# A fused cross-attention block on one core: GpSimd adds the half sums of the softmax once more, VectorE sums 256 columns instead of 512, and the order inside the step changes

## Chip, cores and metric

The kernel runs on one core of a Trainium2 chip. The metric is the device time of one execution in microseconds (us). Shown are the median of three runs, and one profiled execution with its own time.

## What is computed

For each of 16 batches, 1024 query rows of 512 numbers attend to 64 context rows, with 16 heads of 32:

```python
xq  = ada_ln(x_q,  t_vec, Wss_q,  bss_q)
xkv = ada_ln(x_kv, t_vec, Wss_kv, bss_kv)
q      = (xq @ Wq + bq).reshape(B, Lq, nh, dh)
k, v   = split((xkv @ Wkv + bkv).reshape(B, Lkv, 2, nh, dh))
attn   = softmax(einsum('bqhd,bkhd->bhqk', q, k) / sqrt(dh), axis=-1)
out    = einsum('bhqk,bkhd->bqhd', attn, v).reshape(B, Lq, H)
return x_q + (out @ Wp + bp)
```

The change touches the sum inside the softmax: for each row and head, 64 exponentials are added up.

## The kernel before

The query rows are cut into 128 units of 128 rows, 8 units to a batch. Products are made in float16 with each operand split into a high and a low half, so three products stand for one.

After a start of some 125 us (modulation, keys and values of all batches, the first units) the kernel is a software pipeline. One step `step(b, i)` handles the unit `i` of batch `b` and, at the same time, later and earlier units. Each engine has its own list of parts for a step, written by hand, and works it off in that order. An engine that waits in one part holds up everything behind it on its list. The engines meet only by semaphores. In step i:

- TensorE (PE): scores of unit i (`score`, L1465), weights times values of unit i-3 (`weigh`, L1487), query projection (`project`, L1442), transposition of the normalised rows of unit i+8 (`turn_x`, L1425), output projection of unit i-3 (`project_out`, L1503). `weigh` waits for both halves of the transposed weights (`pT_landed`) and for the low halves of the rows turned in the step before (`xT_done`). The change leaves PE's list as it is.
- VectorE (DVE): maximum of the scores (`score_max`, L1091), low half of the weights of unit i-2 (`split_p`, L1107), `turned_o` (L1058), scores minus maximum (`softmax_shift`, L1099), sum of unit i-1 (`weight_sums`, L1066), `turned_x` (L1051), reciprocal (`denominators`, L1073), low half of the queries (`query`, L1116), division by the sum (`normalise_p`, L1083).
- ScalarE (ACT): high half of the weights (`split_p`, L691), `turned_o` (L651), output copy (`output`, L667), row sums and squares (L710, L717), `query` (L702), `turned_x` (L643), exponentials (L726), and in steps 2 to 5 the high half of the next batch's weights (`scaled_wq_hi`).
- GpSimd (POOL): bias onto the residual row (`residual`, L503), `half_sums` of unit i-1 (L534), which adds the two halves of the 64 exponentials of each head (512 sums from 1024), the row statistics (`moments`: L479, L482), in steps 3 to 6 `scaled_wq_lo` (L541) and in steps 2 to 5 `scaled_wq` (L517) for the next batch, `add_rows` (output plus residual, L527), `normalise` (rows of unit i+9, L494).
- SyncE (SP) issues all transfers of a step from one queue: the two transposing transfers of the weights of unit i-2 (`turn_p`, L358), the residual row (`load_xr`, L342), the store of unit i-4 (L348), the rows of unit i+12 (`load_x`, L327). Step 7 begins with four copies of the next batch's keys (`copy_keys`, L369), step 2 with two of the values (`copy_values`, L380).

`load_xr(i-1)` waits until the store of unit i-5, which used the same buffer, has landed. `load_x(i+12)` waits for POOL's `normalise` of unit i+8. `copy_keys` waits for the scores of step 7. The steps of batches 1 to 13 run in a loop on the compute engines; the others are written out.

Of the kernel before, what the change touches and what calls it, by code (L numbers as in the profile page):

```python
# [5 lines left out]
ALU = mybir.AluOpType  # L6
# [8 lines left out]
P = 128  # L15
# [6 lines left out]
def adaln_cross_attention(nc, x, ctx_in, cond, Wq, bq, Wkv, bkv, Wp, bp, Wss_q, bss_q, Wss_kv, bss_kv, out):  # L22
# [19 lines left out]
    with ExitStack() as ctx:  # L42
        def sb(name, shape, dt, stack=ctx):
            return stack.enter_context(nc.sbuf_tensor(name, shape, dt))
# [4 lines left out]
        def sem(name):  # L49
            return ctx.enter_context(nc.semaphore(name))  # L50
# [105 lines left out]
        with ExitStack() as scratch:  # L156
# [3 lines left out]
        ctx_kept = sb("ctx_kept", [P, 2 * H], F32)  # L160
# [62 lines left out]
        half_done, den_done, rden_done, norm_done, pv_mm, oT_hi_done, oT_done = (  # L223
            sem(n) for n in ("half_done", "den_done", "rden_done", "norm_done", "pv_mm", "oT_hi_done", "oT_done"))
# [72 lines left out]
        def _(sp):  # L297
# [84 lines left out]
            def step(b, i):  # L382
                if i == 7:
                    copy_keys(b + 1)
                if i == 2 and b > 0:
                    copy_values(b)
                turn_p(b, i - 2, 0)
                turn_p(b, i - 2, 1)
                load_xr(b, i - 1)
                store(b, i - 4)  # L390
                load_x(b, i + 12)
# [41 lines left out]
        def _(pool):  # L433
# [95 lines left out]
            def half_sums(b, off):  # L529

                if exists(b, off):
                    wait(pool, exp_done, upto(b, off))
                    wait(pool, den_done, unit(b, off))
                    pool.tensor_tensor(half_den[:, :, :], pr[:, off % 2, :, 0:LKV // 2], pr[:, off % 2, :, LKV // 2:LKV],  # L534
                                       ALU.add).then_inc(half_done, 1)

# [20 lines left out]
            def step(b, i):  # L557
                residual(b, i - 4)
                await_rows(b, i + 9)
                half_sums(b, i - 1)  # L560
                moments(b, i + 9)
                await_moments(b, i + 9)
                if 3 <= i <= 6:
                    scaled_wq_lo(b + 1, i - 3)
                if 2 <= i <= 5:
                    scaled_wq(b + 1, i - 2)
                add_rows(b, i - 4)
                normalise(b, i + 9)

            def prime():  # L570
# [36 lines left out]
                half_sums(0, 0)  # L607
                half_sums(0, 1)
                key_lo(6)
# [8 lines left out]
        def _(act):  # L618
# [117 lines left out]
            def step(b, i):  # L736
                split_p(b, i - 2)
                turned_o(b, i - 3)
                output(b, i - 4)
                if i == 4:  # L740
                    query_bias(b + 1)
                sum_rows(b, i + 10)
                query(b, i + 4)
                turned_x(b, i + 8)
                sum_squares(b, i + 10)
                exponential(b, i)
                if 2 <= i <= 5:
                    scaled_wq_hi(b + 1, i - 2)
# [138 lines left out]
        def _(dve):  # L887
# [173 lines left out]
            def weight_sums(b, off):  # L1061

                if exists(b, off):
                    wait(dve, half_done, upto(b, off))
                    wait(dve, rden_done, unit(b, off))
                    dve.tensor_reduce(den[:, :], half_den[:, :, :], AX_X, ALU.add).then_inc(den_done, 1)  # L1066
# [52 lines left out]
            def step(b, i):  # L1119
                score_max(b, i)  # L1120
                split_p(b, i - 2)
                turned_o(b, i - 3)
                softmax_shift(b, i)
                weight_sums(b, i - 1)
                turned_x(b, i + 8)
                denominators(b, i - 1)
                query(b, i + 4)
                normalise_p(b, i - 1)

# [477 lines left out]
```

## Time and profile before

| | |
|---|---|
| median of 3 runs | 1062.99 us (1062.55 to 1064.18) |
| profiled execution: its time | 1062.06 us |
| profiled execution: its span | 1060.2 us |
| busy in the span: PE, DVE, POOL, ACT | 1019.4, 989.8, 832.3, 787.5 us |
| mean granted clock of TensorE | 0.994 of full speed |

The span runs from the first to the last instruction of the profiled execution; its time is 1.9 us longer, and the median 0.9 us above that. Busy time is a union of intervals on one engine; matmuls overlap, and their ends are modelled, so a PE that is always busy is not by that alone at its peak. The chain that ended last goes through PE for 75% of the span, through transfers for 7% and through SP's queue for 7%.

### The profile page before, as it was taken

The numbers are of one execution on the slowest core, as the hardware profiler recorded it, in microseconds if no ns is written. First come the engines' busy times: TensorE is split into PE (matmuls) and PEld (weight loads), VectorE is DVE, ScalarE is ACT, GpSimd is POOL, SyncE is SP. The second block draws the span as 40 slices with busy tenths as digits, with TensorE's granted clock in tenths as the row PEclk, the third lists the DMA queues.
The fourth block names the chain that finished last, engine by engine and source line by source line (L and its number), as shares of the span: only waits on it lengthen the run. The fifth ranks groups of instructions, "written<-read, shape, count | busy, mean of one in ns | idle before, by whom it ended". The sixth has DMA issues, their size and how long they took to land.

```text
span 1060.2 us, 29080 instructions
## 1 busy us (share of the span) xinstructions
PE 1019.4 (96%) x10051; PEld 576.6 (54%) x10051; DVE 989.8 (93%) x1288; ACT 787.5 (74%) x1400; POOL 832.3 (79%) x933
## 2 busy tenths in 40 slices
PE   6999899999999999999999999999999999999965
PEld 2666555555555555555555555555555555555532
DVE  5775899999999999999999999999999999999994
ACT  2564677878787887878787878878787878877552
POOL 2372587979888897979898888979797988889454
PEclk8999999999999999999999999999999999999999
DMA  9231478877777778777777777777777777776775
GB/s 346 102 100 51 99 175 190 178 191 183 182 193 175 184 172 197 184 176 188 194 174 183 189 182 189 169 194 183 177 188 185 183 191 177 184 191 142 160 159 129
DMA packets 382386, 185.19 MB, mean 175 GB/s; under 512 B 324828, under 2 KB 328952, under 8 KB 382344
## 3 DMA queue, kind: packets, MB, share of 16 engines
q1 hardware_dynamic: 382320, 184.66, 71.4%
q8 instruction: 22, 0.36, 0.1%
q14 instruction: 20, 0.16, 0.1%
q10 hardware_dynamic: 24, 0.01, 0.0%
HBM read 77.90 MB, written 33.55 MB: 105 GB/s over the span
## 4 chain that ended last, share of the span: by engine, by line
PE 75%; DMA 7%; SPq 7%; DVE 4%; issue 4%; POOL 2%; ACT 0%; POOLq 0%; DVEq 0%; ACTq 0%
PE ps_q L1442 26%; PE ps_o L1503 26%; PE ps_s L1465 8%; PE ps_v L1487 8%; DMA pt<-p 6%; PE ps_v L1425 4%; SPq L369 3%; SPq L358 2%; DMA cx<-in_ctx_dram 1%; PE ps_v L1296 1%; SPq L334 1%; DVE v L1023 1%; DVE p L1107 0%; DVE cx L932 0%; PE ps_s L1367 0%
## 5 line engine op out<-in xcount | busy, mean ns | idle before, releaser
L527 POOL TENSOR_TENSOR xr<-y,xr 128x512 f32<-128x512 f32 x128 | 163.0, 1273 | 57.5 <-ACT y L667 55.7
L691 ACT CAST p<-ps_t 128x1024 f16<-128x1024 f32 x128 | 129.5, 1012 | 100.0 <-DVE ps_t L1083 98.3
L534 POOL TENSOR_TENSOR half_den<-pr 128x512 f32<-128x512 f32 x128 | 163.4, 1277 | 51.1 <-ACT pr L726 49.0
L503 POOL TENSOR_TENSOR xr<-xr,bp_row 128x512 f32<-128x512 f32 x128 | 163.0, 1273 | 0.8 <-DMA xr<-in_x_dram 0.8
L1091 DVE TENSOR_REDUCE mx<-ps_s 128x16 f32<-128x1024 f32 x128 | 156.8, 1225 | 7.1 <-PE ps_s L1465 2.8
L1107 DVE TENSOR_TENSOR p<-ps_t,p 128x1024 f16<-128x1024 f32 x128 | 156.6, 1223 | 4.0 <-ACT p L691 2.7
L1083 DVE SCALAR_TENSOR_TENSOR ps_t<-pr,ps_v 128x1024 f32<-128x1024 f32 x128 | 155.8, 1217 | 0.3
L1099 DVE TENSOR_TENSOR pr<-ps_s,mx 128x1024 f32<-128x1024 f32 x128 | 155.6, 1215 | 0.1
L726 ACT ACTIVATE pr<-pr,exp_scale 128x1024 f32<-128x1024 f32 x128 | 146.3, 1143 | 10.6 <-DVE pr L1099 10.6
L702 ACT ACTIVATE q_hi<-ps_q,cur_bq 128x512 f16<-128x512 f32 x126 | 86.6, 687 | 89.1 <-PE ps_q L1442 89.1
L1503 PE MATMUL ps_o<-wp_hi,oT_hi 128*128 128x512 f16 x512 | 132.3, 381 | 13.5 <-DVE oT_lo L1058 13.5
L1503 PE MATMUL ps_o<-wp_lo,oT_hi 128*128 128x512 f16 x512 | 132.0, 380 | 0.0
L1503 PE MATMUL ps_o<-wp_hi,oT_lo 128*128 128x512 f16 x512 | 131.4, 379 | 0.0
L1442 PE MATMUL ps_q<-xT_hi,w_hi 128*128 128x512 f16 x504 | 130.7, 382 | 0.0
L1442 PE MATMUL ps_q<-xT_hi,w_lo 128*128 128x512 f16 x504 | 129.3, 379 | 0.0
L1442 PE MATMUL ps_q<-xT_lo,w_hi 128*128 128x512 f16 x504 | 129.3, 379 | 0.0
L1487 PE MATMUL ps_v<-pt,vb 128*64 128x128 f16 x3072 | 110.2, 221 | 9.5 <-DMA pt<-p 8.6
L1465 PEld LDWEIGHTS ps_s<-kb,q_hi 64*128 64x128 f16 x2048 | 80.5, 94 | 54.3 <-issue 46.6
L1465 PE MATMUL ps_s<-kb,q_hi 64*128 64x128 f16 x2048 | 108.0, 217 | 0.0
L1487 PEld LDWEIGHTS ps_v<-pt,vb 128*64 128x64 f16 x3072 | 90.2, 110 | 24.8 <-issue 14.0
L494 POOL TENSOR_SCALAR xh<-x_in,neg_mean,rstd 128x512 f32<-128x512 f32 x124 | 96.1, 775 | 1.5 <-POOL rstd L482 1.5
L1058 DVE TENSOR_TENSOR oT_lo<-ps_v,oT_hi 128x512 f16<-128x512 f32 x128 | 87.2, 681 | 6.5 <-ACT oT_hi L651 6.5
(211 smaller groups left out, 1878.4 us busy)
## 6 DMA issues: line engine op xcount, KB each, us to landing
x_in<-in_x_dram SPq DMA_DIRECT2D x128, 256.0 KB, 3.2
xr<-in_x_dram SPq DMA_DIRECT2D x128, 256.0 KB, 3.1
out_dram<-xr SPq DMA_DIRECT2D x128, 256.0 KB, 3.1
pt<-p SPq DMA_TRANSPOSE x256, 3.2
raw<-in_L_xcond_Wss_kv_dram SPq DMA_DIRECT2D x4, 512.0 KB, 5.9
cx<-in_ctx_dram SPq DMA_DIRECT2D x4, 512.0 KB, 10.9
wss_q_raw<-in_L_xcond_Wss_q_dram SPq DMA_DIRECT2D x4, 512.0 KB, 10.9
raw<-in_L_xcond_Wkv_dram SPq DMA_DIRECT2D x2, 1024.0 KB, 13.8
```

What stands on the lines that cost most here:

```text
L503: pool.tensor_tensor(xr[:, s, :], xr[:, s, :], bp_row[:, :], ALU.add).then_inc(xr_ready, 1)
L527: pool.tensor_tensor(xr[:, s, :], y[:, off % 2, :], xr[:, s, :], ALU.add).then_inc(y_ready, 1)
L534: pool.tensor_tensor(half_den[:, :, :], pr[:, off % 2, :, 0:LKV // 2], pr[:, off % 2, :, LKV // 2:LKV], ALU.add).then_inc(half_done, 1)
L726: act.activation(pr[:, off % 2], pr[:, off % 2], ACT.Exp, scale=exp_scale[:, 0:1])\
L1083: dve.scalar_tensor_tensor(out=weights, in0=pr[:, off % 2, :, :], scalar=P_UNIT, in1=rden[:, :].unsqueeze(2).to_broadcast([P, NH, LKV]), o ...
L1091: dve.tensor_reduce(mx[:, :], scores, AX_X, ALU.max).then_inc(mx_done, 1)
L1099: dve.tensor_tensor(pr[:, off % 2, :, :], scores, mx[:, :].unsqueeze(2).to_broadcast([P, NH, LKV]), ALU.subtract).then_inc(sub_done, 1)
L1107: dve.tensor_tensor(p16[:, 1, :, :], weights, p16[:, 0, :, :], ALU.subtract).then_inc(p_split, 1)
L1442: last = pe.matmul(bank[:, :], w[:, k, cols], xt[:, s, k, :], start=(n == 0), stop=(n == 3 * KC - 1))
L1465: last = pe.matmul(ps_s[:, e, P * m:P * (m + 1)], q[rows, s, m, cols], kb[rows, part, m, :, :].rearrange("p h l -> p (h l)"), start=(n == ...
L1487: last = pe.matmul(ps_v[64 * e:64 * (e + 1), 0, P * m:P * (m + 1)], vb[:, part, 2 * m + e, :, :].rearrange("p h c -> p (h c)"), pt[:, p_pa ...
L1503: last = pe.matmul(ps_o[:, :], ot[:, k, :], w[:, k, :], start=(n == 0), stop=(n == 3 * KC - 1))
```

## The change

`half_sums` stays, and a second addition on POOL follows it, `quarter_sums`: it adds the halves of the half sums (256 sums from 512) into a new buffer. VectorE's `weight_sums` then sums 256 columns. POOL's `half_sums` of a unit waits for the quarter sums of the unit before, no longer for VectorE's sum. Beside that the lists of SP, POOL, ACT and DVE get another order. PE's list stays.

```diff
+        quarter_den = sb("quarter_den", [P, NH, LKV // 4], F32)
...
             def step(b, i):
+                load_x(b, i + 12)
                 if i == 7:
                     copy_keys(b + 1)
+                load_xr(b, i - 1)
+                turn_p(b, i - 2, 0)
+                turn_p(b, i - 2, 1)
                 if i == 2 and b > 0:
                     copy_values(b)
-                turn_p(b, i - 2, 0)
-                turn_p(b, i - 2, 1)
-                load_xr(b, i - 1)
                 store(b, i - 4)
-                load_x(b, i + 12)
...
                 if exists(b, off):
                     wait(pool, exp_done, upto(b, off))
-                    wait(pool, den_done, unit(b, off))
+                    wait(pool, quarter_done, unit(b, off))
                     pool.tensor_tensor(half_den[:, :, :], pr[:, off % 2, :, 0:LKV // 2], pr[:, off % 2, :, LKV // 2:LKV],
                                        ALU.add).then_inc(half_done, 1)
+            def quarter_sums(b, off):
+                if exists(b, off):
+                    if isinstance(b, int) and unit(b, off) == 0:
+                        pool.wait_ge(v_mm, KC)
+                        pool.wait_ge(k_mm, KC)
+                    wait(pool, half_done, upto(b, off))
+                    wait(pool, den_done, unit(b, off))
+                    pool.tensor_tensor(quarter_den[:, :, :], half_den[:, :, 0:LKV // 4], half_den[:, :, LKV // 4:LKV // 2],
+                                       ALU.add).then_inc(quarter_done, 1)
...
             def step(b, i):
+                await_rows(b, i + 9)
                 residual(b, i - 4)
-                await_rows(b, i + 9)
+                moments(b, i + 9)
                 half_sums(b, i - 1)
-                moments(b, i + 9)
                 await_moments(b, i + 9)
+                quarter_sums(b, i - 1)
+                add_rows(b, i - 4)
                 if 3 <= i <= 6:
                     scaled_wq_lo(b + 1, i - 3)
+                normalise(b, i + 9)
                 if 2 <= i <= 5:
                     scaled_wq(b + 1, i - 2)
-                add_rows(b, i - 4)
-                normalise(b, i + 9)
...
             def step(b, i):
+                if i == 4:
+                    query_bias(b + 1)
+                output(b, i - 4)
                 split_p(b, i - 2)
                 turned_o(b, i - 3)
-                output(b, i - 4)
-                if i == 4:
-                    query_bias(b + 1)
                 sum_rows(b, i + 10)
+                sum_squares(b, i + 10)
                 query(b, i + 4)
+                exponential(b, i)
                 turned_x(b, i + 8)
-                sum_squares(b, i + 10)
-                exponential(b, i)
...
-                    wait(dve, half_done, upto(b, off))
+                    wait(dve, quarter_done, upto(b, off))
                     wait(dve, rden_done, unit(b, off))
-                    dve.tensor_reduce(den[:, :], half_den[:, :, :], AX_X, ALU.add).then_inc(den_done, 1)
+                    dve.tensor_reduce(den[:, :], quarter_den[:, :, :], AX_X, ALU.add).then_inc(den_done, 1)
...
                 weight_sums(b, i - 1)
-                turned_x(b, i + 8)
                 denominators(b, i - 1)
                 query(b, i + 4)
                 normalise_p(b, i - 1)
+                turned_x(b, i + 8)
```

SP's queue in step 7 of a batch, before and then with the change (kb: the next batch's keys; pt: the transposed weights; xr: the residual row; x_in: rows to come):

```order
L369 DMA kb<-k 32x8x64 [waits k_ready,s_mm]
L369 DMA kb<-k 32x8x64 x3
L358 DMA_TRANSPOSE pt<-p 128x8x128 [waits p_hi_done,pv_mm]
L358 DMA_TRANSPOSE pt<-p 128x8x128 [waits p_split]
L342 DMA xr<-in_x_dram 128x512 [waits stored2]
L348 DMA out_dram<-xr 128x512 [waits y_ready]
L327 DMA x_in<-in_x_dram 128x512 [waits xh_ready]
```

```order
L328 DMA x_in<-in_x_dram 128x512 [waits xh_ready]
L370 DMA kb<-k 32x8x64 [waits k_ready,s_mm]
L370 DMA kb<-k 32x8x64 x3
L343 DMA xr<-in_x_dram 128x512 [waits stored2]
L359 DMA_TRANSPOSE pt<-p 128x8x128 [waits p_hi_done,pv_mm]
L359 DMA_TRANSPOSE pt<-p 128x8x128 [waits p_split]
L349 DMA out_dram<-xr 128x512 [waits y_ready]
```

The loads of x_in and xr moved from behind the two transposing transfers to ahead of them; that of xr stands between the key copies and the transposing transfers.

POOL's list in a step with work for the next batch's weights (steps 3 to 5), before and then with the change:

```order
L503 TENSOR_TENSOR xr<-xr,bp_row 128x512 [waits xr_loaded1,bias_ready]
L534 TENSOR_TENSOR half_den<-pr 128x512 [waits den_done,exp_done,row_stats]
L479 TENSOR_SCALAR veps<-row_sq 128x1
L482 TENSOR_TENSOR rstd<-veps,half_neg 128x1 [waits ln_step]
L541 TENSOR_TENSOR w_lo<-w_tmp,w_hi 128x4x128 [waits w_hi_done]
L517 TENSOR_TENSOR w_tmp<-wq,cur_sc 128x512 [waits w_done]
L527 TENSOR_TENSOR xr<-y,xr 128x512 [waits xr_ready,y_copied]
L494 TENSOR_SCALAR xh<-x_in,neg_mean,rstd 128x512
```

```order
L504 TENSOR_TENSOR xr<-xr,bp_row 128x512 [waits xr_loaded1,bias_ready,row_stats]
L480 TENSOR_SCALAR veps<-row_sq 128x1
L483 TENSOR_TENSOR rstd<-veps,half_neg 128x1 [waits ln_step]
L535 TENSOR_TENSOR half_den<-pr 128x512 [waits quarter_done,exp_done]
L546 TENSOR_TENSOR quarter_den<-half_den 128x256 [waits half_done,den_done,ln_step,xT_turned]
L528 TENSOR_TENSOR xr<-y,xr 128x512 [waits xr_ready,y_copied]
L553 TENSOR_TENSOR w_lo<-w_tmp,w_hi 128x4x128 [waits w_hi_done]
L495 TENSOR_SCALAR xh<-x_in,neg_mean,rstd 128x512
L518 TENSOR_TENSOR w_tmp<-wq,cur_sc 128x512 [waits w_done]
```

One addition of 256 columns is new, directly behind the half sums and waiting for them; the row statistics moved ahead of the half sums, and the work for the weights behind `add_rows`.

DVE's list from the sum on, before and then with the change:

```order
L1066 TENSOR_REDUCE den<-half_den 128x16 [waits rden_done,half_done]
L1051 TENSOR_TENSOR xT_lo<-ps_v,xT_hi 128x4x128 [waits xT_hi_done]
L1073 RECIPROCAL ps_v<-den 128x16 [waits norm_done,den_done]
L1116 SCALAR_TENSOR_TENSOR q_lo<-ps_q,cur_bq,q_hi 128x512 [waits q_hi_done]
L1083 SCALAR_TENSOR_TENSOR ps_t<-pr,ps_v 128x1024 [waits p_split,rden_done]
```

```order
L1081 TENSOR_REDUCE den<-quarter_den 128x16 [waits rden_done,quarter_done]
L1088 RECIPROCAL ps_v<-den 128x16 [waits norm_done,den_done]
L1131 SCALAR_TENSOR_TENSOR q_lo<-ps_q,cur_bq,q_hi 128x512 [waits q_hi_done]
L1098 SCALAR_TENSOR_TENSOR ps_t<-pr,ps_v 128x1024 [waits p_split,rden_done]
L1066 TENSOR_TENSOR xT_lo<-ps_v,xT_hi 128x4x128 [waits xT_hi_done]
```

The low half of the turned rows went from between the sum and its reciprocal to the end of the step.

## Rows read from the trace of the kernel before

**Rows 1.** Busy time by stretch: us, PE, PEld, DVE, ACT, POOL (count), clock, DMA share, GB/s.
```profile
500.00:600.00 100.00, 99.69 (x1037) 56.18 (x1034) 99.20 (x123) 79.72 (x144) 85.70 (x97) 1.00 0.77 185
```

**Rows 2.** Timeline of one step, PE and DVE: start us, us, engine, line, operation.
```profile
500.01 0.86 PE L1487 MATMUL ps_v<-pt,vb 128*64 128x128 f16 x24
500.12 1.23 DVE L1091 TENSOR_REDUCE mx<-ps_s 128x16 f32<-128x1024 f32 x1
...
504.20 0.68 DVE L1066 TENSOR_REDUCE den<-half_den 128x16 f32<-128x512 f32 x1
...
505.41 0.25 DVE L1073 RECIPROCAL ps_v<-den 128x16 f32<-128x16 f32 x1
...
506.16 1.22 DVE L1083 SCALAR_TENSOR_TENSOR ps_t<-pr,ps_v 128x1024 f32<-128x1024 f32 x1
...
507.30 0.86 PE L1487 MATMUL ps_v<-pt,vb 128*64 128x128 f16 x24
```

**Rows 3.** Waits of PE between 200 and 900 us: total, times, longest.
```profile
PE ps_v L1487 <- DMA pt<-p: 1.7, 9, 0.3
```

**Rows 4.** Chain that ended last, around step 7 of two batches: start us, us, what.
```profile
506.59 0.80 PE ps_s L1465 x24
...
511.47 3.22 DMA pt<-p
514.69 0.14 issue
...
565.15 0.80 PE ps_s L1465 x24
```

**Rows 5.** SP's queue in the same step 7, with the store before it.
```profile
505.87 0.34 SPq L348 DMA_DIRECT2D out_dram<-xr  x1
...
507.40 2.65 SPq L369 DMA_DIRECT2D kb<-k  x4
510.15 2.66 SPq L358 DMA_TRANSPOSE pt<-p  x2
512.85 0.58 SPq L342 DMA_DIRECT2D xr<-in_x_dram  x1
...
513.95 0.43 SPq L327 DMA_DIRECT2D x_in<-in_x_dram  x1
```

**Rows 6.** Waits of POOL between 200 and 900 us.
```profile
POOL half_den L534 <- ACT pr L726: 35.7, 48, 1.1
POOL xr L527 <- ACT y L667: 20.7, 24, 0.9
POOL w_lo L541 <- POOL rstd L482: 10.5, 48, 0.2
```

**Rows 7.** Timeline of POOL in one step.
```profile
507.79 1.28 POOL L534 TENSOR_TENSOR half_den<-pr 128x512 f32<-128x512 f32 x1
509.15 0.19 POOL L479 TENSOR_SCALAR veps<-row_sq 128x1 f32<-128x1 f32 x1
509.43 0.55 POOL L482 TENSOR_TENSOR rstd<-veps,half_neg 128x1 f32<-128x1 f32 x1
```

**Rows 8.** Issue to landing of L358 between 127 and 131 us.
```profile
DMA to landing us min/median/max: 3.6/3.7/3.7
```

**Rows 9.** Issue to landing of L348 (stores) in the whole span.
```profile
DMA to landing us min/median/max: 2.0/3.1/4.6
```

**Rows 10.** Timeline of PE at the first steps of the pipeline.
```profile
133.65 0.86 PE L1487 MATMUL ps_v<-pt,vb 128*64 128x128 f16 x24 [2.61 <-DMA pt<-p]
```

**Rows 11.** Timeline of the last units: ACT, PE, SP.
```profile
1043.00 1.01 ACT L691 CAST p<-ps_t 128x1024 f16<-128x1024 f32 x1 [2.61 <-DVE ps_t L1083]
...
1044.07 1.03 PE L1503 MATMUL ps_o<-wp_hi,oT_lo 128*128 128x512 f16 x4
...
1045.92 2.61 SPq L358 DMA_TRANSPOSE pt<-p  x2
```

More of the change, by code:

```diff
@@ L159, in adaln_cross_attention @@
         p16 = sb("p16", [P, 2, NH, LKV], F16)
-        ctx_kept = sb("ctx_kept", [P, 2 * H], F32)
+        quarter_den = sb("quarter_den", [P, NH, LKV // 4], F32)
+        ctx_kept = sb("ctx_kept", [P, 2 * H - NH * LKV // 4], F32)
         ctx_kept1 = sb("ctx_kept1", [P, KC, 512], F32)
@@ L222, in adaln_cross_attention @@
             sem(n) for n in ("s_mm", "mx_done", "sub_done", "exp_done", "p_hi_done", "p_split"))
-        half_done, den_done, rden_done, norm_done, pv_mm, oT_hi_done, oT_done = (
-            sem(n) for n in ("half_done", "den_done", "rden_done", "norm_done", "pv_mm", "oT_hi_done", "oT_done"))
+        half_done, quarter_done, den_done, rden_done, norm_done, pv_mm, oT_hi_done, oT_done = (
+            sem(n) for n in ("half_done", "quarter_done", "den_done", "rden_done", "norm_done", "pv_mm", "oT_hi_done", "oT_done"))
         out_mm, xr_ready, y_copied, y_ready = sem("out_mm"), sem("xr_ready"), sem("y_copied"), sem("y_ready")
@@ L607, in prime @@
                 half_sums(0, 0)
+                quarter_sums(0, 0)
                 half_sums(0, 1)
+                quarter_sums(0, 1)
                 key_lo(6)
```

## The prediction

> **What bounds the kernel now.** I read the busy time by stretch first. In the middle of the run PE is busy 99.69 of 100 us, DVE 99.20, POOL 85.70 and ACT 79.72 [rows 1]: two engines look full, so busy shares do not tell which one paces. The timeline of one step does. From one `weigh` to the next PE takes 507.30 - 500.01 = 7.29 us [rows 2], and the waits of PE over 700 us come to 1.7 us, in nine places, all for the transposed weights [rows 3]. DVE has work for nearly the same 7.29 us, but no wait of PE is for DVE. So PE's own work of 7.29 us a step, 58.32 us for the 8 steps of a batch, is a floor that the change, which leaves PE's list alone, cannot lower.
>
> The chain shows what is above the floor. From the scores of step 7 of one batch to those of the next are 565.15 - 506.59 = 58.56 us [rows 4], 0.24 us over the floor. They are lost behind step 7: SP issues four key copies (507.40, 2.65 us), only then the two transposing transfers (510.15) [rows 5]; the second is issued at 511.47, lands 3.22 us later, and 0.14 us after that `weigh` starts [rows 4]. **So VectorE's saving has 0.24 us a batch to win, 3.6 us over the 15 changes from one batch to the next.** The question is what the rest of the change costs.
>
> **The change part by part.** *VectorE.* A sum over 1024 columns takes 1.23 us, one over 512 takes 0.68 [rows 2]; the line through both gives 0.40 for 256, a gain of 0.28 a step (none at all is the one bound, half of 0.68 the other). PE does not wait for it, so by itself I count it zero: PE's 7.29 us cover it. But `turned_x` goes to the end of the step, and its result lets PE's `weigh` of the next step begin. The sum starts 4.08 us after the step's first DVE row; then 0.40, some 0.03 until the dependent reciprocal, 0.75 from there to `normalise_p` as now, 1.22 for that and about 0.6 for the low half: 7.08 us. With 0.14 from signal to `weigh`, as after a landing [rows 4], that is 7.22, where `weigh` wants to start 507.30 - 500.12 = 7.18 us after the same row [rows 2]. Just in time; I take zero and keep the other end (no saving in the sum, 0.3 us late) for a rival.
>
> *GpSimd.* Its 256 column addition is not in the trace. Half of the 512 column one is 0.64 us; the line through that row (1.28) and the one column row (0.19) gives 0.19 + 256 x 1.09/511 = 0.74 us [rows 7]. I take 0.73, since a GpSimd instruction visibly has a fixed part. It waits for the half sums of the same engine: `veps` ends at 509.34 and `rstd`, which needs it, starts at 509.43 [rows 7], so 0.09 (0.22 at worst, the wait of `w_lo` for `rstd`: 10.5 us in 48 waits [rows 6]). That is 0.82 us a step, 6.6 a batch. Has POOL this room? Over 12 batches it waited 35.7 us for exponentials and 20.7 for outputs [rows 6], 4.7 us a batch; so 58.56 - 4.70 = 53.86 us are taken, fixed gaps included. The 10.5 us of `w_lo` waiting for `rstd` (0.88 a batch) go away, because the half sums now stand between. New demand: 53.86 + 6.56 - 0.88 = **59.5 us a batch, more than PE's 58.32**. Bounds: 58.1 (0.64 and no wait) to 61.5 (0.74 and 0.22 each time, nothing hidden). The waits can be used up nearly in full, since ACT's output copy now comes first in its step, and the exponential is moved ahead of `turned_x`. POOL becomes the pacing engine, at +0.98 us a batch over 58.56; in steps 3 to 5, which carry the weights' work, its sums fall behind and VectorE's sum waits for them.
>
> Here a rule bears on the result. By busy time POOL takes 85.70% of 58.56 us [rows 1], 50.2, and with eight times 0.74 it is 56.1: POOL would fit, and nothing of the 14.7 us below would come from it. By the spacing of starts it does not. The Trainium skill (Perfetto Trace Analysis, GPSIMD Engine Instruction) says that the reported spans of this engine are unreliable and that the distance from start to start is to be used; the trace shows why: half sums last 1.28 us and the next start comes after 1.36 [rows 7]. I go by spacing, and keep the other as a rival.
>
> *SyncE.* In step 7 the load of the residual row now stands between the key copies and the transposing transfers: 0.58 us and 0.04 of issue gap, 0.62 later [rows 5]. The key copies cannot start earlier, as they wait for step 7's scores; `load_x` ahead of them is 0.43 us, and POOL's late `normalise` can hold it. The landing gets longer too: with two such loads just ahead it took 3.6 to 3.7 us [rows 8] instead of 3.22 [rows 4]. Half of the difference, 0.22, is my value. So PE loses 0.84 a batch here (0.62 to 1.07). In the other steps the same loads are ahead, and the residual's load waits for the store of the step before to land: issued at 505.87 [rows 5], landing 3.1 later [rows 9], load 0.62, first transfer 1.3: the second is issued at about 510.95. At 511.47 it was 0.24 too late, so 511.23 is the last moment: 0.28 us of room, zero taken. The value copies of step 2, moved behind the transfers, have a step's rest; zero as well.
>
> *Adding up.* POOL's 0.98 and SP's 0.84 a batch are delays of two loops beside each other, PE's being late gives POOL time; I take the larger one: 15 x 0.98 = 14.7. At the first step of the pipeline, where PE already waits 2.61 us for the transposed weights [rows 10], SP now issues both loads ahead of them: 0.43 + 0.58 + 0.08 = 1.1. At the end ACT's copy of an output comes ahead of the last unit's weights: PE ends that output at 1045.10, the copy is some 0.7, the weights' high half starts at 1045.8 instead of 1043.00, ends a microsecond later, and SP's transfers, at 1045.92 before, start at about 1046.8 [rows 11]: 0.85 (between 0 and 2.8). Sum: 14.7 + 1.1 + 0.85 = 16.6 us on the profiled execution's 1062.06, **1079 us**; against the median of 1062.99 it is 16 us.
>
> **Rivals.** *SP's delay alone.* POOL's addition fits. Then 15 x 0.84 + 1.9 = 14.5 gives 1076.6, with 0.62 it is 1073.3. For it speaks POOL's busy share; against it that its gaps fill every step with `scaled_wq`.
>
> *Transfers late in every step.* The Trainium skill (DMA: Bandwidth & Descriptors, Queues, rings and completion order) says that each transfer engine takes its descriptors in ring order; loads issued ahead are then served ahead. The trace agrees in part: 3.7 instead of 3.2 us behind two loads. With the whole 0.45 in every step the room of 0.28 is gone and seven steps lose 0.17 each, step 7 loses 1.07: 2.26 a batch, 1062.06 + 33.9 + 1.9 = 1098. If VectorE's sum does not get shorter at all, so that the change does not do what it says, `turned_x` ends 0.3 us late; a late `weigh` delays the next step too, so half of it counts, 0.16 a step, 1.3 a batch beside SP's 0.84: 1096. Both decide by rows that are off by a few tenths; the half landing penalty alone keeps 0.06 us of room.
>
> *Faster.* PE's only wait goes: the second transposing transfer of step 7 would have to be issued by 511.23 instead of about 512.1, or land in 2.4 us instead of 3.22. Then 3.6 us are won, 1058.5. Nothing in the rows is that short; only that PE is full now bounds it from the other side.
>
> *No change.* POOL fits, and SP's issue of the residual load is hidden by a wait that I read wrongly (0.24 a batch stays): 1061 to 1065.
>
> **Numbers.** Forecast 0.50; SP alone 0.22; late in every step 0.13; no change 0.07; faster 0.08. The range 1061 to 1094 leaves out the faster case and the upper half of the late one. About 0.2% (2 us) is what a measurement of this kernel can tell from no change. Slower 0.85, same 0.07, faster 0.08.
>
> **What would show it.** Right: POOL's waits for exponentials and outputs shrink from 4.7 us a batch to nearly nothing; the step 7 to step 7 distance grows to about 59.5; VectorE waits for the quarter sums in steps 5 to 7; PE waits for the transposed weights after step 7 by 0.8 us or more; the sum takes 0.40 us. Wrong: PE's step stays at 7.29 with waits of POOL left, or PE waits in every step for the transposed weights or for VectorE's low half.

## The result and the profile after

The changed kernel takes 1094.27 us (median of 4 runs, 1091.85 to 1096.03) beside 1062.77 us of the kernel before (4 runs, 1061.79 to 1064.18): 1.0292 times as long, 95% interval 1.0276 to 1.0308. It is slower, as forecast, but by 31.5 us where the forecast was 16. The profiled execution, the fastest of the four, took 1091.85 us; its span is 1090.0 us (1060.2 before), the mean granted clock 0.992 (0.994 before).

Busy time in the middle of the run, to set beside [rows 1]; the columns are the same:

```profile
500.00:600.00 100.00, 98.02 (x1002) 54.68 (x1001) 93.58 (x120) 80.31 (x143) 94.21 (x109) 1.00 0.74 177
```

TensorE went from 99.69 to 98.02, VectorE from 99.20 to 93.58, and GpSimd from 85.70 to 94.21. Nothing reads 100 any more. Next, TensorE's `weigh` rows (L1502 is L1487 of before) over one batch of the changed kernel, from the timeline:

```profile
529.05 0.86 PE L1502 MATMUL ps_v<-pt,vb 128*64 128x128 f16 x24 [0.54 <-DMA pt<-p]
...
536.34 0.86 PE L1502 MATMUL ps_v<-pt,vb 128*64 128x128 f16 x24
...
543.73 0.86 PE L1502 MATMUL ps_v<-pt,vb 128*64 128x128 f16 x24
...
551.19 0.86 PE L1502 MATMUL ps_v<-pt,vb 128*64 128x128 f16 x24
...
558.48 0.86 PE L1502 MATMUL ps_v<-pt,vb 128*64 128x128 f16 x24
...
565.88 0.86 PE L1502 MATMUL ps_v<-pt,vb 128*64 128x128 f16 x24
...
573.17 0.86 PE L1502 MATMUL ps_v<-pt,vb 128*64 128x128 f16 x24
...
581.05 0.86 PE L1502 MATMUL ps_v<-pt,vb 128*64 128x128 f16 x24 [0.17 <-issue]
...
588.98 0.86 PE L1502 MATMUL ps_v<-pt,vb 128*64 128x128 f16 x24 [0.57 <-DMA pt<-p]
```

From one row to the next should be the 7.29 us of [rows 2]. Six of the eight distances are within 0.17 of it, and two are long: 7.88 and 7.93, from the seventh `weigh` to the eighth and from the eighth to the first of the next batch. The batch is 588.98 - 529.05 = 59.93 us. The second long one ends a wait for the transposed weights; what lies behind the first the chain of waits shows, in the same stretch:

```profile
571.61 1.05 POOL w_tmp L518
...
573.21 0.68 ACT y L682
573.90 0.91 ACT p L706
...
574.92 0.43 DVE p L1122
...
576.07 0.69 DVE oT_lo L1073
...
576.89 0.63 PE ps_v L1440 x4
577.52 2.59 PE ps_o L1518 x12
580.11 0.79 PE ps_s L1480 x24
...
580.92 0.66 SPq L370
...
583.60 0.60 SPq L343
...
585.63 3.22 DMA pt<-p
...
588.98 0.86 PE ps_v L1502 x24
```

GpSimd's preparation of the weights (`w_tmp`, now last in its step) ends late; ScalarE, which makes the weights' high half from it, comes late to the next output and split of p; VectorE gets its low halves later, TensorE its next turn of x, the scores of step 7 follow, then SP's four key copies (L370), then the residual row (L343), then the transposes. **GpSimd's delay and SP's delay lie on one chain, one behind the other**, not on two loops beside each other.

The waits of TensorE, to set beside [rows 3], and those of GpSimd, beside [rows 6] (total us, times, longest; 200 to 900 us):

```profile
PE ps_v L1502 <- DMA pt<-p: 7.6, 13, 0.9
PE ps_v L1440 <- DVE oT_lo L1073: 2.3, 11, 0.3
PE ps_v L1502 <- issue: 2.0, 12, 0.2
```
```profile
POOL quarter_den L546 <- POOL half_den L535: 21.6, 94, 0.2
POOL half_den L535 <- ACT pr L741: 2.5, 11, 0.2
POOL xr L504 <- ACT junk L732: 2.0, 8, 0.5
```

Of GpSimd's 56.4 us of waits for ScalarE, 4.5 are left: 0.38 a batch. It is nearly full, though its busy time is 94%. One of these waits, 0.23 us, is the last row of the next block, 12.75 us behind the late `weigh` of 529.05. The addition itself, from its timeline (beside [rows 7]), and VectorE's shorter sum (beside [rows 2]):

```profile
528.67 1.28 POOL L535 TENSOR_TENSOR half_den<-pr 128x512 f32<-128x512 f32 x1
530.17 0.73 POOL L546 TENSOR_TENSOR quarter_den<-half_den 128x256 f32<-128x256 f32 x1 [0.23 <-POOL half_den L535]
530.87 1.27 POOL L528 TENSOR_TENSOR xr<-y,xr 128x512 f32<-128x512 f32 x1
...
541.80 1.26 POOL L535 TENSOR_TENSOR half_den<-pr 128x512 f32<-128x512 f32 x1 [0.23 <-ACT pr L741]
```
```profile
562.59 0.41 DVE L1081 TENSOR_REDUCE den<-quarter_den 128x16 f32<-128x256 f32 x1
```

From the half sums to the next instruction was 1.36 us and is now 530.87 - 528.67 = 2.20: the addition costs GpSimd 0.84 us a step, where the prediction had 0.82.

For the sum, the issues of the key copies mark the batches. In the twelve between the second and the fourteenth issue a batch took (940.75 - 221.03) / 12 = 59.98 us; before it was 58.56. So 12 x 1.42 = 17.0 of the profiled 29.8 us were lost there. The rest is at the ends: 2.33 up to the first key copies (157.95 against 155.62), 4.15 in the first interval (63.08 against 58.93), 2.97 in the last (61.68 against 58.71), 3.34 behind it (87.57 against 84.23). A batch's own 1.42 is in two of these figures once more; without it the start lost 2.33 + 2.73 = 5.06 us and the end 1.55 + 3.34 = 4.89, beside 14 x 1.42 = 19.9 in the batches.

### The profile page after: what moved, and what is told of

It reads as the page before. It is cut to its first block, busy times and chain, and to the rows that moved or that the text cites. A ratio compares the mean times of both kernels' runs of the same rounds, so it can differ in the third digit from the quotient of the medians.

```text
span 1090.0 us, 29335 instructions
## 1 busy us (share of the span) xinstructions
PE 1028.6 (94%) x10051; PEld 578.9 (53%) x10051; DVE 958.6 (88%) x1288; ACT 807.5 (74%) x1400; POOL 918.2 (84%) x1061
## 4 chain that ended last, share of the span: by engine, by line
PE 35%; POOL 28%; issue 15%; SPq 7%; DMA 6%; DVE 4%; ACT 4%; POOLq 1%; ACTq 0%; DVEq 0%
PE ps_o L1518 12%; PE ps_q L1457 11%; POOL xr L504 6%; POOL half_den L535 6%; POOL xr L528 5%; DMA pt<-p 5%; PE ps_v L1502 4%; POOL w_tmp L518 4%; PE ps_s L1480 4%; POOL w_lo L553 3%; SPq L370 3%; PE ps_v L1440 2%; SPq L359 2%; POOL xh L495 1%; ACT p L706 1%
## 5 line engine op out<-in xcount | busy, mean ns | idle before, releaser
L682 ACT ACTIVATE y<-ps_o,unscale 128x512 f32<-128x512 f32 x128 | 87.9, 687 | 76.9 <-PE ps_o L1518 73.1
L1502 PE MATMUL ps_v<-pt,vb 128*64 128x128 f16 x3072 | 110.8, 221 | 26.4 <-DMA pt<-p 22.3
L546 POOL TENSOR_TENSOR quarter_den<-half_den 128x256 f32<-128x256 f32 x128 | 94.2, 736 | 28.0 <-POOL half_den L535 27.1
L1502 PEld LDWEIGHTS ps_v<-pt,vb 128*64 128x64 f16 x3072 | 92.2, 110 | 43.8 <-issue 38.0
```

Source lines behind the costliest of these rows:

```text
L1502: last = pe.matmul(ps_v[64 * e:64 * (e + 1), 0, P * m:P * (m + 1)], vb[:, part, 2 * m + e, :, :].rearrange("p h c -> p (h c)"), pt[:, p_pa ...
```

## The experiments

Each kernel is compared with the kernel before on the same chip; the medians come from several chips, so the rows are set beside each other by the ratio. "Batch" is the mean of the same twelve intervals between key copies, "first copies" the issue of the first ones, both of the profiled execution.

| kernel | median us | ratio to before, 95% | batch us | first copies us |
|---|---|---|---|---|
| before (first comparison) | 1062.77 | 1 | 58.56 | 155.62 |
| changed | 1094.27 | 1.0276 to 1.0308 | 59.98 | 157.95 |
| e1: SP's order alone | 1082.54 | 1.0152 to 1.0211 | 59.62 | 159.42 |
| e2: addition, all orders of before | 1091.05 | 1.0223 to 1.0285 | 60.55 | 157.70 |
| e3: changed, SP's order of before | 1075.68 | 1.0091 to 1.0151 | 59.49 | 154.48 |
| e4: changed without the addition | 1098.73 | 1.0297 to 1.0362 | 60.32 | 160.38 |
| e5: changed, residual rows behind | 1084.73 | 1.0199 to 1.0234 | 59.94 | 156.69 |
| e6: changed, weights' work earlier | 1095.87 | 1.0280 to 1.0334 | 59.97 | 159.44 |
| e8: before, turned x last on VectorE | 1078.00 | 1.0127 to 1.0166 | 59.80 | 156.76 |
| e9: e4 with SP's order of before | 1078.58 | 1.0141 to 1.0190 | 59.81 | 154.81 |
| e10: changed, only SP's read of x first | 1080.19 | 1.0128 to 1.0180 | 59.48 | 158.74 |
| e11: e1, value copies ahead again | 1085.62 | 1.0189 to 1.0241 | 59.79 | 159.33 |
| c1: before, new start | 1063.07 | 0.9989 to 1.0019 | 58.56 | 155.85 |
| c2: c1, one key copy by ScalarE | 1058.53 | 0.9935 to 0.9970 | 58.32 | 157.09 |

**Taking the change apart: e1 to e4.** SP's order alone on the kernel before (e1), and the changed kernel with SP's old order (e3), are the same edit in two directions:

```diff
             def step(b, i):
+                load_x(b, i + 12)
                 if i == 7:
                     copy_keys(b + 1)
-                if i == 2 and b > 0:
-                    copy_values(b)
+                load_xr(b, i - 1)
                 turn_p(b, i - 2, 0)
                 turn_p(b, i - 2, 1)
-                load_xr(b, i - 1)
+                if i == 2 and b > 0:
+                    copy_values(b)
                 store(b, i - 4)
-                load_x(b, i + 12)
```

Expected of e1:

> Edit: the kernel before with SP's new order alone (reads of x first, residual rows between key copies and transposes, value copies behind the transposes). Theory A (GpSimd's added sum and SP's delay lie one behind the other in one loop a batch, so that they add): SP alone makes the batch longer by what the residual rows' issue puts ahead of step 7's transposes, 0.6 to 0.9 us, so 59.2 to 59.5 us between key copies and about 1062.8 + 15 x 0.75 = 1074 us; GpSimd, with 0.9 us of room a batch, follows. Theory B (GpSimd's load alone sets the changed kernel's batch and SP's delay lies beside it): SP alone costs the same here, 1072 to 1077, but then putting SP back in the changed kernel (another run) gives nothing. Theory C (SP's new order hurts the start and the end too): the first key copies come 2 us later than before, and the total is over 1080.

Measured: 59.62 us a batch and 1082.54 us, more than theories A and B said; the first copies are 3.8 us late, as C said. TensorE's rows of e1, a step 7 and a step 2, and its waits:

```profile
577.45 0.86 PE L1487 MATMUL ps_v<-pt,vb 128*64 128x128 f16 x24
...
585.66 0.86 PE L1487 MATMUL ps_v<-pt,vb 128*64 128x128 f16 x24 [0.84 <-DMA pt<-p]
...
600.24 0.86 PE L1487 MATMUL ps_v<-pt,vb 128*64 128x128 f16 x24
...
607.92 0.86 PE L1487 MATMUL ps_v<-pt,vb 128*64 128x128 f16 x24 [0.32 <-DMA vb<-v_all]
```
```profile
PE ps_v L1487 <- DMA pt<-p: 10.5, 13, 0.9
PE ps_v L1487 <- DMA vb<-v_all: 3.5, 11, 0.3
```

Two transfers are late, each once a batch. The `weigh` behind step 7 comes 585.66 - 577.45 = 8.21 us after the last one, 0.92 over 7.29; before it was 0.24 over, so the residual rows' issue costs 0.68 here. The other is the copy of the values, put behind step 2's transposes: 607.92 - 600.24 = 7.68, 0.39 over. Together 1.07, the batch's 1.06.

Expected of e3:

> Edit: the changed kernel with SP's order of before. Theory A: SP's 0.6 to 0.9 us leave the batch, 59.9 becomes 59.0 to 59.4 us, GpSimd's demand is then the floor, and the time falls by 9 to 15 us to 1079 to 1085; if start and end stay late (about 10 us of the loss) it is not lower. Theory B: no change, 1092 to 1096. Theory C (SP's order makes the late start and end): also the first copies come back to 155.6 us, and the time falls to 1070 to 1078.

Measured: 59.49 us a batch, just above A's range; 1075.68 us, faster than A said and within C's range, since the start and the end came back too. GpSimd has one row of waits left in the whole stretch, for its own result:

```profile
POOL quarter_den L546 <- POOL half_den L535: 21.9, 95, 0.2
```

An engine that waits for nobody paces the kernel: GpSimd's demand is 59.49 us a batch. And the first copies come even earlier than in the kernel before. SP's order is worth 1.0292 - 1.0121 = 0.017 of the time in the changed kernel and 0.018 in the kernel before. **The two parts add in the total**: 0.0121 for the rest and 0.0182 for SP's order make 0.0303, and 0.0292 was measured. In the batches alone they do not add in full (0.93 and 1.06 us make 1.42), and the ends make up for it.

e2 keeps the addition and takes back every order; the second addition stands behind the wait for the moments.

```diff
                 await_moments(b, i + 9)
+                quarter_sums(b, i - 1)
                 if 3 <= i <= 6:
                     scaled_wq_lo(b + 1, i - 3)
```

> Edit: the changed kernel with the orders of all four lists of before, and the second addition on GpSimd behind the wait for the moments. Theory A: GpSimd's demand is the same 59.5 us a batch, but without SP's delay in the loop; the batch is 58.9 to 59.5 us and the time 1069 to 1077. Theory B: GpSimd alone sets the changed kernel's pace, so the batch is 59.9 us as in the changed kernel and the time 1085 to 1094. Theory D (the orders alone make the loss, the addition fits): 1061 to 1065.

Measured: 60.55 us a batch, outside every theory; the time lies in B's range, but not by B's batch of 59.9. VectorE now waits for the quarter sums, a row that the changed kernel does not have, though the sum stands at the same place of VectorE's list in both; which of the new orders takes the wait away was not isolated:

```profile
DVE den L1081 <- POOL quarter_den L546: 26.5, 36, 1.4
```

GpSimd itself waits 16.7 us for exponentials in 23 places, 1.4 a batch: 60.55 less 1.4 is 59.15, so its demand is no higher than in e3. In the old orders its lateness comes back to it as waiting. The new orders are worth 1.06 us a batch to the addition.

e4 keeps all orders and takes the addition out (VectorE sums 512 columns again).

> Edit: the changed kernel without the second addition (VectorE sums 512 columns of the half sums again), all new orders kept. Theory A: SP's delay stays, GpSimd's 0.82 us a step go, so the batch is 59.2 to 59.5 us and the time 1074 to 1080, a little over SP alone by the late start and end of the other orders. Theory B (GpSimd's added work is the whole loss): 1061 to 1066. Theory D (the orders alone make the loss): 1090 to 1095.

Measured: 60.32 us a batch, 1098.73 us, the slowest of all and nearest to D: in the batch the orders without the addition lose more than with it (in the whole time the two intervals touch). TensorE waits 9.7 us for the transposes in 12 places, as with SP's order alone, and in addition:

```profile
PE ps_v L1499 <- DVE xT_lo L1063: 9.0, 35, 0.3
```

That is VectorE's low half of the transposed x, which its new order puts last. The prediction has this lateness as a rival, for a sum that does not get shorter; none of e4's theories had it. e8 and e9 price it.

**VectorE's order: e8 and e9.** e8 moves this one call in the kernel before; e9 is e4 with SP's order of before.

```diff
                 weight_sums(b, i - 1)
-                turned_x(b, i + 8)
                 denominators(b, i - 1)
                 query(b, i + 4)
                 normalise_p(b, i - 1)
+                turned_x(b, i + 8)
```

> Edit: the kernel before with one thing moved, the low half of the transposed x at the end of VectorE's step. Theory E: the same late rows, a wait of TensorE of 0.1 to 0.3 us in most steps; 59.2 to 59.8 us a batch, 1072 to 1083. Rival F2 (it is late only together with ScalarE's new order, which also puts its high half at the end): 58.5 to 58.8 us a batch, 1061 to 1067.

> Edit: the kernel before with the new orders of GpSimd, ScalarE and VectorE, without the second addition, and SP's order of before. Theory E (turned x at the end of VectorE's step comes too late when the sum still takes 0.68 us; the second addition pays for that place by the 0.28 us that it saves): TensorE waits for the low half of the transposed x in every second step by 0.2 to 0.3 us, 59.4 to 59.7 us a batch, 1076 to 1083. Rival F (the orders of these three engines cost nothing without SP's): 58.5 to 58.7 us a batch, 1060 to 1066.

Measured: 59.80 and 59.81 us a batch, 1078.00 and 1078.58 us: theory E in both, with e9's batch 0.1 above its range. Three of e8's rows:

```profile
530.61 0.86 PE L1487 MATMUL ps_v<-pt,vb 128*64 128x128 f16 x24 [0.38 <-DVE xT_lo L1051]
...
537.90 0.86 PE L1487 MATMUL ps_v<-pt,vb 128*64 128x128 f16 x24
...
545.55 0.86 PE L1487 MATMUL ps_v<-pt,vb 128*64 128x128 f16 x24 [0.29 <-DVE xT_lo L1051]
```

It is late in every second step only; 59.80 - 58.56 = 1.24 us a batch, 0.155 a step on the mean. In the changed kernel and in e3 the row does not appear: the shorter sum (0.41 us where it was 0.68) pays for the place, at least down to GpSimd's pace of 59.49, below which no kernel with this order and the addition was run. So the saving that the change is made for is spent on an order that the change itself brought, and ScalarE's and GpSimd's new orders cost nothing beside it (e9's batch is e8's).

**GpSimd's order: e6.** Is it `w_tmp` at the end of GpSimd's step, for which ScalarE waits 12.6 us in 12 places, that adds the 0.59 us of the first long step?

```diff
                 quarter_sums(b, i - 1)
-                add_rows(b, i - 4)
                 if 3 <= i <= 6:
                     scaled_wq_lo(b + 1, i - 3)
-                normalise(b, i + 9)
                 if 2 <= i <= 5:
                     scaled_wq(b + 1, i - 2)
+                add_rows(b, i - 4)
+                normalise(b, i + 9)
```

> Edit: the changed kernel with both preparations of the next batch's query weights ahead of the addition of the residual rows and of the normalising on GpSimd. Theory A2: GpSimd's list only changes its order, its demand stays at 59.48 us a batch; the wait of ScalarE for the prepared weights (12.6 us in 12 steps) goes, the transposed x comes later; the batch stays within 0.2 us of 59.96 and the time within 1089 to 1098. Rival D2 (that ScalarE holds the output and the split behind the late weights is what adds 0.4 to 0.6 us at one step of each batch): 59.4 to 59.6 us a batch, 1083 to 1088.

Measured: 59.97 us a batch, 1095.87 us, as theory A2 said. The rival falls. ScalarE's wait for the weights is gone from the rows, the lateness is not: TensorE's waits for the transposes grew from 7.6 to 12.2 us, and one step of 8.39 to 8.41 us stands where two long ones were. The chain through `w_tmp` is the path that GpSimd's overload took, not its source.

**SP's order in parts: e5, e10, e11.** In the changed kernel, e5 puts `load_xr` behind the two transposes, and e10 in addition `copy_values` ahead of them, so that only `load_x` stays first. e11 is e1 with `copy_values` ahead.

```diff
-                load_xr(b, i - 1)
                 turn_p(b, i - 2, 0)
                 turn_p(b, i - 2, 1)
+                load_xr(b, i - 1)
                 if i == 2 and b > 0:
                     copy_values(b)
```

> Edit: the changed kernel with the residual-row read put back behind the two transposes on SP; the read of x stays first and the value copies stay behind. Theory A2 (GpSimd, which never waits for another engine when SP has its old order, holds 59.48 us a batch, and SP's delay ahead of step 7's transposes is added where GpSimd waits): the transposes are ready in time again, GpSimd alone paces, 59.4 to 59.6 us a batch in place of 59.96; 14 x 0.45 = 6 us less in the batches, and 2 to 6 us less at the start if the residual rows (and not the read of x) made it late: 1080 to 1087. Rival B2 (the read of x ahead of the transposes is what costs): no more than 2 us gained, 1091 to 1095. Rival C2 (the value copies behind the transposes cost, as with SP alone, 0.4 us a batch): the batch stays at 59.8 or more.

> Edit: the changed kernel with the residual-row read behind the transposes and the value copies ahead of them, as before; of SP's new order only the read of x ahead of everything stays. Theory A3 (SP's order makes two transfers late, each once a batch: step 7's transposes behind the residual rows, and the value copies behind step 2's transposes; where one is taken away the other takes its place): both waits go, GpSimd alone paces as with SP's old order, 59.4 to 59.6 us between key copies and 1073 to 1079 us. Rival C3 (the read of x in front costs too): 59.7 to 60.0 us a batch, 1080 to 1088.

> Edit: the kernel before with SP's new order, but the value copies ahead of the transposes, as before. Theory A3: the wait for the value copies (0.40 us a batch with SP's order alone) goes and the wait for step 7's transposes (0.88) stays: 59.6 falls to 59.1 to 59.3 us a batch, the time by 5 to 7 us from 1082.5 to 1074 to 1078. Rival G (the copies and the residual rows in front of step 2's transposes, 1.9 us of issue, make those late instead): 59.5 us or more, 1080 to 1086.

e5: 59.94 us a batch, nothing gained there. The wait moved to the value copies, which now stand behind one more issue (rival C2):

```profile
PE ps_v L1502 <- DMA vb<-v_all: 12.4, 11, 1.6
```

What e5 gains on the changed kernel, 1.0292 - 1.0217 or some 8 us, comes from the ends: its first interval is 60.30 us where the changed kernel's is 63.08. So its time lies in theory A2's range, but not by A2's shorter batch.

e10: both transfers back in time, 59.48 us a batch: GpSimd's pace again, with no other wait of GpSimd than for its own result, as in e3. Theory A3 holds for the batches. But the time, 1080.19 us, is above its range: 1.0154 to e3's 1.0121, some 3.5 us. Its four runs go from 1077.10 us at a mean granted clock of 0.992 to 1081.51 at 0.987. The profiled execution is 6.0 us longer than e3's: 4.3 up to the first copies and 1.9 behind the last ones. The read of x in front costs nothing in the batches, only at the ends, and 2.6 of the 4.3 us are the clock's, as the last section shows.

e11: rival G. With values and residual rows ahead of step 2's transposes these come late instead (0.40 to 0.45 us, beside 0.77 to 0.88 behind step 7): 59.79 us, more than e1. In these two steps, whatever stands behind the read of the residual rows in SP's queue is late.

**A version that is faster than both: c1 and c2.** The rows of before left 0.24 us a batch and a start of some microseconds. c1 issues the second unit's transposes ahead of the last placements of values; c2 in addition gives one of the four key copies to ScalarE's queue.

```diff
             place_values(6)
+            turn_p(0, 1, 0)
+            turn_p(0, 1, 1)
             load_x(0, 14)
             place_values(7)
...
-            for f in range(2):
+            for f in range(3):
                 load_xr(0, f)
-            for i in range(3, PER):
+            store(0, -1)
+            load_x(0, 15)
+            for i in range(4, PER):
```
```diff
             def copy_keys(b):
...
-                for j in range(HPG):
+                for j in range(HPG - 1):
...
+            def copy_last_keys(b):
...
+                act.wait_ge(s_mm, PER * b)
+                act.wait_ge(k_ready, CT)
+                j = HPG - 1
+                rows = slice(DH * j, DH * (j + 1))
+                act.dma_start(kb[rows, :, :, j % 2, :], k16[rows, b, :, :, :]).then_inc(kb_in, 16)
...
                 sum_rows(b, i + 10)
+                if i == 7:
+                    copy_last_keys(b + 1)
                 query(b, i + 4)
```

> Edit: the kernel before with the second unit's transposes issued ahead of the last reads and value placements of the start, and nothing else. Theory H (at the start TensorE waits 2.6 us for these transposes because 3.9 us of issues stand in front of them on SP): the wait goes, the first key copies come at 153 in place of 155.6 us, the batches stay at 58.56: 1059 to 1061 where the kernel before takes 1062 to 1063. Rival I (the work put behind becomes late in its place, or the weights of the value path are what lands late): within 0.1% of the kernel before.

> Edit: the kernel before with the same new start, and with one of the four key copies of each batch issued by ScalarE, between its row sums and its query, where it waits 0.71 us for TensorE. Theory J (SP's four key copies in front of step 7's transposes are the only thing that keeps the kernel before off TensorE's floor of 58.32 us a batch): the wait of 0.24 us goes, 58.30 to 58.35 us a batch, 15 x 0.24 = 3.6 us less than with the new start alone: 1055 to 1058. Rival K (the issue costs ScalarE more than its idle 0.71 us, or the transposes land later because the copy beside them takes the rings): 58.5 us a batch or more, no faster than the new start alone.

c1: no change, rival I. The wait went from the second `weigh` to the third, behind transposes that now stand after the work put back (2.15 us at 140.26), and 1.06 more at 163.27. c2: 58.32 us a batch, TensorE's floor to the hundredth, and 1058.53 us, 0.5 above J's range and faster than before by 0.30 to 0.65%. The whole of TensorE's waits between 200 and 900 us, and the copy on ScalarE's queue beside its work:

```profile
PE ps_v L1503 <- DMA pt<-p: 0.2, 1, 0.2
```
```profile
566.28 0.59 ACT L655 CAST oT_hi<-ps_v 128x512 f16<-128x512 f32 x1
566.52 0.62 ACTq L681 DMA_DIRECT2D kb<-k  x1
```

The issue lies beside a running copy and takes no visible time from ScalarE; it comes ahead of the row sums (567.34) that stand before it on the list, and not in the wait of 0.71 us that was meant for it. Since c1 gained nothing and c2's first copies are 1.5 us later than before, the key copy without the new start might be a little better still; that was not tried.

## Why the prediction was right and wrong

- **TensorE's floor of 58.32 us and 0.24 over it**: right. c2 reaches 58.32 when the four copies in front of the transposes are three.
- **GpSimd's demand, 59.5 us a batch**: right. e3 and e10, where it waits for nobody, give 59.49 and 59.48. The addition takes 0.736 us on the mean of 128 (0.73 taken); its wait for its own half sums is 0.23 (0.09 taken, 0.22 the bound). That the forecast holds all the same is in part luck: the next row starts at 530.87, before the addition's reported end at 530.90, where a gap of 0.08 was before, so the two cost 0.84 a step (0.82 taken). By busy time it would have fitted: in 59.90 us of e3 (from 521.02) GpSimd is busy 56.64 and TensorE 59.19, and yet GpSimd is the one that waits for nobody. The rule of the Trainium skill (Perfetto Trace Analysis, GPSIMD Engine Instruction), to go by the distance of starts on this engine and not by its spans, agrees with these rows.
- **SP's issue of the residual rows, 0.62 a batch**: right, 0.68 in e1's rows. **Its landing, 0.22 longer**: wrong. Behind step 7 the landing stays at 3.22 us in the changed kernel's chain, as in [rows 4]; the 3.7 of [rows 8] belong to the start, where four copies of values (from 124.79) stand ahead besides the two loads. The sign of 0.8 us or more of waiting behind step 7 did not come either: the rows above have 0.54 and 0.57.
- **The value copies, "zero as well"**: wrong. With SP's order alone they cost 0.39 a batch, in e5 more (the changed kernel's own rows show no wait for them). They "have a step's rest" was argued from the list, without a row for when `weigh` of the next batch wants them.
- **VectorE's saving zero, `turned_x` "just in time"**: right as far as GpSimd's slower pace lets it be seen, and e8 shows how narrowly: without the saving 0.155 us a step, where the rival's price was 0.16.
- **"I take the larger one"**: this step failed. The prediction set GpSimd's 0.98 and SP's 0.84 on two loops beside each other. They measured 0.93 (e3) and 1.06 (e1, of which 0.39 are the value copies), and together 1.42: more than the larger, less than the sum of 1.99. The chain shows why: SP's key copies wait for scores that wait for what GpSimd made late, and SP's late transposes make GpSimd wait again. Its waits for ScalarE stand in the changed kernel and are gone in e3 and e10, where SP's transfers are in time. GpSimd's 59.49 and the 0.38 a batch that it still waits for ScalarE make 59.87 of the 59.98. So the batches lost 19.9 us where 14.7 were forecast: 5.2 of the 13.2 us by which the profiled execution missed its forecast of 1078.7.
- **VectorE waits for the quarter sums in steps 5 to 7**: did not appear in the changed kernel; it does in e2. With the new orders the lateness reaches TensorE through ScalarE.
- **The start, 1.1 us**: the place was right, the size not: 5.06, of which 2.33 up to the first copies. **The end, 0.85**: the copy of the output ahead of the weights costs about that, since e3, which has the same ScalarE order, takes 84.96 us behind the last copies where before took 84.23, 0.73 more; but the changed kernel lost 4.89. (e3 has the other new orders too, so that price is not isolated.) The missing 4.0 us at either side are the other 8 of the 13.2. e5, which only puts the read of the residual rows back behind the transposes, gets some 8 us back at the ends, so most of it hangs on that read; the last section shows where it is lost.
- **The range, 1061 to 1094**: the measured median stands at its upper end, which was drawn to take in half of the case of transfers late in every step. The sum that gave 1079 does not lead there; that the range reaches so far is luck.

## What to carry to other kernels

Before taking the larger of two delays, follow the chain once around: if what the second waits for is made by what the first delays, they add, in full or in part, and only the idle time of the pacing engine says by how much. An engine that waits for nobody is the pace, whatever its busy share; an engine that looks full may have exactly the slack that an order gives it, and a saving there can be spent by moving a call. In a queue that is full in one step of a batch, a read that is moved ahead makes late what now stands behind it, whichever transfer that is; giving one issue to another engine's queue took the wait away.

## What was not expected of the hardware

**Some waits were followed by half the clock.** At the start [rows 10] show 2.61 us of TensorE waiting, and the granted clock stayed 1.00. In the changed kernel SP issues two reads ahead of the same transposes, and the wait is 4.33 us. Busy time by stretch; the granted clock stands behind the five busy times:

```profile
130.30:134.60 4.30, 0.00 (x0) 0.02 (x1) 1.23 (x2) 1.78 (x3) 3.90 (x6) 0.95 1.06 266
134.60:136.00 1.40, 1.39 (x24) 1.26 (x24) 1.22 (x1) 0.00 (x0) 1.40 (x2) 0.50 0.65 241
136.00:138.00 2.00, 2.00 (x8) 0.78 (x7) 1.24 (x2) 1.83 (x4) 2.00 (x3) 0.61 0.34 68
```

0.50 is 1.2 GHz. The step behind this wait takes 143.27 - 134.61 = 8.66 us, 1.37 over 7.29, so the wait cost 1.72 us more than that of before by itself and 1.37 by the clock, which is back at 1.00 from 138 us on. In e10, with only the read of x in front, the wait was 3.43 us, and the rows behind it are slow for longer:

```profile
134.17 1.49 PE L1502 MATMUL ps_v<-pt,vb 128*64 128x128 f16 x24 [3.43 <-DMA pt<-p]
135.59 1.89 PE L1457 MATMUL ps_q<-xT_hi,w_hi 128*128 128x512 f16 x4
137.27 1.91 PE L1457 MATMUL ps_q<-xT_lo,w_hi 128*128 128x512 f16 x4
```

The step is 144.05 - 134.17 = 9.88 us, 2.59 over. `weigh` came 0.52 us after that of [rows 10], the next one 3.11 after that of before, and so do the first copies, 3.12: most of this late start is the clock's, not the queue's. In e5, whose lists are e10's up to there, the wait was 3.33 us, the granted clock stayed 1.00, and the step took 142.01 - 134.72 = 7.29 us. A wait alone does not tell whether the clock falls: it did behind 2.24 us in the changed kernel, and not behind 3.33 in e5, 2.61 in the kernel before or 2.15 in c1.

**Three transposes landed late beside a load of program code, and the load alone does not explain it.** In the changed kernel three `weigh` waited over 2 us after the start, at the first change of batch and at the last two:

```profile
167.45 0.86 PE L1502 MATMUL ps_v<-pt,vb 128*64 128x128 f16 x24 [2.24 <-DMA pt<-p]
...
950.65 0.86 PE L1502 MATMUL ps_v<-pt,vb 128*64 128x128 f16 x24 [2.41 <-DMA pt<-p]
...
1012.21 0.86 PE L1502 MATMUL ps_v<-pt,vb 128*64 128x128 f16 x24 [2.43 <-DMA pt<-p]
```

Their second transposes landed 4.6 to 4.9 us after issue, where it was 3.2 to 3.4 in two other batches (224.4 and 584.3 us). In each of the three stretches, and in neither of those two, the DMA view has a transfer of the queue for instructions, here at 947.5 to 948.0 us, between the issue and the landing:

```profile
q8 instruction: 1, 0.02, 16.8%
```

For the first of the three, the transfer engines then stood nearly idle: 4 to 10 GB/s from 165.5 to 166.4 us, while the transposes had not landed. The kernel before loads code there too (at 163.6 and 925.2 us), but just after its transposes had landed. The three waits are 1.67, 1.84 and 1.86 us longer than the 0.57 of an ordinary batch, and behind the first the clock fell again (step of 8.98 us, 1.69 over). The sum is 7.1 us; start and end lost 9.95, and 6.9 of that is not in the first 2.33 or in ScalarE's 0.73.

The code load alone does not hold the transposes. In e1, e3, e5 and e10 it also falls between the issue and the landing at the first change of batch (in e3 at 161.0 us, with the issue at 158.6 and the landing at 161.9), and these transposes landed 3.2 to 3.4 us after issue. The late landings are in the three kernels that have both the read of the residual rows ahead of the transposes and the new orders of the other engines: the changed one, e4 (waits of 2.56, 2.66 and 2.32 us) and e6 (2.56, 3.05 and 2.15). e1 has the read ahead but the old orders, and waits 0.85, 1.12 and 0.66 us at the same places; e5 has the new orders but the read behind, and waits 0.20, 0.29 and 0.21. So the three late landings hang on that read together with the other orders; what holds the transposes there stays open.
